# A decoder layer with routed experts: shared and expert tiles in another order, and the last sort spread differently

## What is computed

```python
probs = softmax(xf @ gate_w.T)
top_w, top_idx = top_k(probs, 4)
top_w = top_w / sum(top_w)
combine = zeros((T, 16)).at[rows, top_idx].set(top_w)
act = silu(einsum('td,ehd->teh', xf, w1)) * einsum('td,ehd->teh', xf, w3)
moe_out = einsum('ted,te->td', einsum('teh,edh->ted', act, w2), combine)
shared = silu(xf @ sw1.T) * (xf @ sw3.T) @ sw2.T
x = layernorm(x + moe_out + shared)
```

## Time and profile before

| | before |
|---|---|
| median of three runs | 969.44 us |
| lowest, highest | 969.18, 972.33 us |
| the profiled execution, device time | 975.99 us |
| its span in the trace | 973.7 us |
| mean granted clock of PE | 0.977 |
| busy: PE, PEld, DVE, ACT, POOL | 94%, 51%, 72%, 65%, 28% |

### The profile page before, as it was taken

The page is one execution under the profiler, slowest core; times in us unless marked ns, Lnnn a source line. Parts: engine busy times, 40 slices in busy tenths (PEclk is TensorE's granted clock), DMA queues, the critical chain, the costliest instruction groups (busy, mean ns, idle before and its releaser), DMA issues.

```text
span 973.7 us, 18713 instructions
## 1 busy us (share of the span) xinstructions
PE 914.7 (94%) x6751; PEld 497.8 (51%) x6751; DVE 703.9 (72%) x1121; ACT 635.3 (65%) x1354; POOL 273.9 (28%) x339
## 2 busy tenths in 40 slices
PE   8999999879999999999999999999989999799992
PEld 3455766434444444444444444444433577578771
DVE  2104889889999998898998989998897273211586
ACT  1323343238888888888888888877778755466662
POOL 1006675520000001020000110013444426655564
PEclk9999999869999999999999999999999999989997
DMA  9202956610444321010000000102335424445895
GB/s 328 66 0 82 119 146 133 121 66 3 128 137 132 100 65 26 8 29 24 24 13 24 25 12 24 31 13 89 96 111 170 130 67 122 136 125 160 267 298 172
DMA packets 69837, 93.05 MB, mean 96 GB/s; under 512 B 15254, under 2 KB 52632, under 8 KB 69686
## 3 DMA queue, kind: packets, MB, share of 16 engines
q1 hardware_dynamic: 62068, 70.06, 26.4%
q0 software_dynamic: 6928, 18.82, 5.3%
q10 hardware_dynamic: 752, 2.98, 1.7%
HBM read 50.34 MB, written 39.40 MB: 92 GB/s over the span
## 4 chain that ended last, share of the span: by engine, by line
PE 75%; DVE 11%; DMA 6%; issue 4%; ACT 3%; POOL 1%; SPq 0%; another core or an unknown queue 0%; POOLq 0%; ACTq 0%; DVEq 0%
PE psum L1338 20%; PE psum L1246 16%; PE psum L1324 9%; PE psum L1521 8%; DVE mpart L1675 7%; PE psum L1539 4%; DMA kparts_d<-region 3%; PE psum L1173 3%; PE psum L1140 3%; PE psum L1483 2%; ACT region L1088 2%; PE psum L1196 2%; PE psum L1298 2%; PE psum L1265 1%; PE psum L1360 1%
## 5 line engine op out<-in xcount | busy, mean ns | idle before, releaser
L1088 ACT ACTIVATE region<-psum 128x512 f32<-128x512 f32 (+1 forms) x832 | 448.3, 606 | 102.1 <-PE psum L1324 86.1
L1675 DVE TENSOR_REDUCE mpart<-psum 128x2 f32<-128x1024 f32 x384 | 462.0, 1222 | 37.5 <-PE psum L1246 31.6
L1338 PE MATMUL psum<-region 128*32 128x256 f32 (+1 forms) x3120 | 249.8, 392 | 2.3 <-ACT numT L987 0.6
L1246 PE MATMUL psum<-kstack,qstack 63*128 63x512 f32 (+1 forms) x1024 | 215.2, 448 | 13.4 <-DVE mpart L1675 11.8
L1246 PEld LDWEIGHTS psum<-kstack,qstack 63*128 63x128 f32 x1024 | 89.9, 188 | 184.7 <-issue 129.9
L1324 PE MATMUL psum<-qstack,kstack 64*128 64x512 f32 (+1 forms) x832 | 176.4, 410 | 1.6 <-ACT region L1088 1.0
L1324 PEld LDWEIGHTS psum<-qstack,kstack 64*128 64x128 f32 (+1 forms) x832 | 111.7, 183 | 18.0 <-ACT region L1088 11.3
L1338 PEld LDWEIGHTS psum<-region 128*32 128x32 f32 (+1 forms) x3120 | 62.1, 108 | 111.5 <-issue 80.8
L862 POOL TENSOR_TENSOR attnT<-num_c,den_c 128x512 f32<-128x512 f32 x7 | 9.1, 1303 | 331.6 <-DMA den_c<-den_d 331.6
L812 POOL DMA_INDIRECT given_d<-y_out,x_in x79 | 78.5, 993 | 65.2 <-ACT y_out L1068 47.4
L1521 PE MATMUL psum<-w_all,xT_in 128*128 x316 | 84.6, 391 | 6.4 <-issue 2.9
(11 more groups left out here) (266 smaller groups left out, 929.8 us busy)
## 6 DMA issues: line engine op xcount, KB each, us to landing
x_in<-sorted_d SPq DMA_DIRECT2D x79, 129.0 KB
sorted_d<-x_in SPq DMA_DIRECT2D x6, 1548.0 KB, 7.7
given<-given_d SPq DMA_DIRECT2D x16, 512.0 KB
qstack<-qparts_d SPq DMA_DIRECT2D x96, 64.0 KB, 2.3
qparts_d<-region SPq DMA_DIRECT2D x8, 512.0 KB, 2.8
kparts_d<-region SPq DMA_DIRECT2D x4, 800.5 KB, 14.1
kstack<-kparts_d SPq DMA_DIRECT2D x6, 400.2 KB, 10.3
kstack<-kparts_d ACTq DMA_DIRECT2D x6, 400.2 KB, 12.3
```

The lines of the kernel that those rows point to most:

```text
L1088: act.activation(prob[0:rows_of, s % 3, j, :], ring(n)[0:rows_of], ACT.Exp).then_inc(ring_read, 1)
L1246: mm = pe.matmul(bank(unit_bank(u) + side)[:, at * w:(at + 1) * w], qstack[rows_of, buffer(G), p, t * P:(t + 1) * P], kstack[rows_of, g * ...
L1338: mm = pe.matmul(bank(NUM_BANK)[VW * j:VW * (j + 1), q], vals[0:r, g, kt, j, :], prob[0:r, s % 3, j, q], start=(kt == 0 and half == 0), st ...
L1675: dve.tensor_reduce(mpart[:, G % 2, qt, :, p, n], both, X, ALU.max).then_inc(max_read, 1)
```

## The change

The list `WORK` gets another order. Before: six shared tiles, six expert tiles, eight pairs of a shared and an expert tile, then 42 expert tiles, and two late shared tiles among the last 25 items. After: three shared tiles, fourteen expert tiles, eleven shared tiles, and then the same 42 and the same rest. Item 28 is expert tile 14 in both, so that all items from 28 on are the same. In the first 28 items expert tile 0 moves from item 6 to item 3 and expert tile 13 from item 27 to item 16. The second edit puts the 16 scatters of the last stage into loops 14 to 29, one in each, in place of two in every three loops of 14 to 36.

```diff
-WORK = mixed("s" * 6 + "e" * 6 + "se" * 8 + "e" * 42 + "s" + "e" * 11 + "s" + "e" * 12, _shared, _expert)
+WORK = mixed("s" * 3 + "e" * 14 + "s" * 11 + "e" * 42 + "s" + "e" * 11 + "s" + "e" * 12, _shared, _expert)
...
-        SCATTER_AT = {14 + (3 * k) // 2: divmod(k, TPC) for k in range(TOPK * TPC)}
+        SCATTER_AT = {14 + k: divmod(k, TPC) for k in range(TOPK * TPC)}
```

## The result

| | before | after |
|---|---|---|
| median, us | 970.88 | 981.35 |
| runs, us | 969.18 to 974.96 | 979.45 to 985.11 |
| ratio to before, 95% interval | | 1.0093 [1.0065, 1.0120] |
| span of the profiled execution, us | 973.7 | 979.3 |

The forecast was 972.8 with a range of 964.0 to 977.5. The sign was right, the size wrong: the ratio is worth 9.0 us where 3.4 were forecast.

A forecast was written before the change was run, and what follows sets the result against it. PE, busy 94% of the span, was taken to bound the kernel. A 3.4 us stop at loop 0, with POOL's part set to nothing, gave 969.44 + 3.4 = 972.8 us; range 964.0 to 977.5.

The forecast's parts named there:

- The stop: At loop 0 PE waits for expert tile 0's load of `x_in`: 3.4 us, bounds 2.5 to 4.7.
- The sign named for it: In the profile after, the projection starts near 776.6 in place of 773.16; before 775 would prove the prediction wrong.
- The slots move with PE by the same 3.4 us.: Behind loop 0, the last chunk's norms, gate, ranks and slots hang on the projection and are 3.4 us late.
- no work is added: Front of the list: same tiles, scatters and reads of tile names and owners, so no work added or taken away.
- rival A: Behind loop 0's stop, PE's dense work runs at half clock, some 3.2 us more: 976.0 us; chance 0.20.
- Part 2, POOL: Last stage's scatters, one per loop: POOL is done sooner, but PE gains nothing; set to nothing in the sum.
- The time table: POOL's last sixteen scatters: done 33.5 us after the slots, at 837.5 on the old clock, 11.4 us sooner than before.
- rival B: Near loop 37, POOL's backlog makes PE wait 0.8 to 1.7 us for `x_in`: 974.5 us; chance 0.10.
- Rival C: PE's gaps of 830 to 860 and the fallen clock there, together 9.3 us, mostly go: 966 us, faster; chance 0.20.

The follow-up runs named there:

- four_shared_first: Changed kernel with four shared tiles in front instead of three, and ten behind the fourteen expert tiles; 973.70 us, 1.0009 of the kernel before.
- after_again: The changed kernel, unedited, run once more on the chip of the later runs; 981.88 us, 1.0093 of the kernel before.
- order_only: Changed kernel with the new tile order but the old spacing of the last chunk's scatters; 984.38 us, 1.0084 of the kernel before.
- fill_for_scatter: Changed kernel with a GpSimd fill in place of each of the sixteen last scatters, last chunk's rows left out; 0.9927 of the kernel before.
- marks_only: Changed kernel with the last chunk's eight marks but without its sixteen scatters, its rows left unsorted; 0.9956 of the kernel before.
- stop_alone: pairs_apart with three shared tiles in front instead of four and eleven behind instead of ten; 978.59 us, 1.0056 of the kernel before.
- pairs_apart_extra: pairs_apart with sixteen more scatters into scratch, one per loop in loops 50 to 65 between gives; 995.29 us, 1.0211 of the kernel before.
- pairs_apart: Changed kernel reordered to 4 shared, 7 expert, 10 shared, 49 expert tiles, two scatters per loop in loops 14 to 21; 971.67 us, 0.9976 of before.

## Why the prediction was wrong, step by step

- **The stop** (2.5 to 4.7 us, 3.4 taken). Right, and term by term: 1.2 us until the load is issued (1.3 forecast) and 2.16 from issue to PE's start (2.1). The twelve profiles with three shared tiles in front have 2.56 to 4.46, mean 3.4. Its cause, the load issued behind the attention stage's last scatter, is in the trace (SP's wait of 3.0 us), and with four shared tiles in front the stop is gone. The sign named for it held as well: the projection starts 773.76 - 766.31 = 7.45 us behind the entry, 776.7 on the clock of before, 776.6 forecast. What no sign looked for is growth behind it: from the projection's start to the last product it is 186.8 us against 182.3.
- **"The slots move with PE by the same 3.4 us."** This is the step that failed. They moved by 6.7 and, in the second profile, 4.6. The first missing term is the reads of owners, which I set to nothing with the words "no work is added": PE has to read before expert tile 0 and again before tile 4, and at items 3 and 7 these reads show as 1.04 + 0.83 us where they showed as 0.43 at item 6: 1.4 us. "No work is added" is true of the reads, but it says nothing of whether they stay covered. One loop later is enough to cover them better: in four_shared_first the read at item 4 shows as 0.42 us and the one at item 8 as nothing. The program fits that (the loop ahead of item 3's read is the only one of these without an `outer`, 0.60 us of PE's work), but no run tests it. The second missing term is the clock, which the sum had at nothing and only rival A counted.
- **Rival A, the clock.** True in after, 5.30 - 3.62 = 1.7 us, about half of the 3.2 I gave it, since half clock lasted some 3 us where I had supposed 6.8; not true in after_again, nor in order_only with a stop of 3.57 us. In the twelve profiles with the stop the granted clock of the first 41 us is below 1.00 in seven; in the eight without it, in none. So the fall goes with the stop but doesn't follow from its length: order_only had none behind 3.57, fill_for_scatter had one behind 2.68. Its length varies too: some 3 us in six of the seven, 7 in marks_only. By the rule of the Trainium skill ("TensorE: Matmul & The Clock Gate", HAM oscillation) that was cited under A, a gap of PE behind a DMA wait sends it back to half clock; the traces agree in seven of twelve. Sum of the front: 3.4 + 1.4 + 1.7 = 6.5 of after's 6.7; 2.9 + 1.4 = 4.3 of after_again's 4.6.
- **Part 2, POOL, "set to nothing".** For the spacing it is right, and a little cautious (0.9975). The time table was close: last scatter 31.8 us after the slots, 33.5 forecast. (Its subtraction from before is off by one: 849.91 - 837.5 is 12.4 us, not 11.4; nothing hangs on it.) No backlog reached PE: **rival B** didn't happen, PE has no idle time from 841 to 876. The stalls hold PE up while POOL goes on, which gives POOL time.
- **Rival C, the gaps go.** Wrong way round. The gaps stand where scatters and gives are dense, and shared tiles beside them don't help: 5.91 + 10.84 + 0.00 us idle in 110 us of after, 2.12 + 2.92 + 4.89 in before. Leaving the front out, after has 10.84 against 7.81, 3.0 more (after_again 9.39, 1.6 more; about 0.7 of after's is the tail of the idle time ahead of the slots, which before has in its front), and its clock in the stretch 41 to 75 is 0.90 in both, where before has 1.00 there and 0.90 in the next. So the same sixteen scatters cost somewhat more than before, and the gain that C hoped for didn't exist.
- **The remainder.** By the profiles after is 8.0 and after_again 957.89 - 764.61 - 186.2 = 7.1 us longer, of which 6.7 and 4.6 are in the front and 1.3 and 2.5 behind it. That closes with the 9.0 of the ratio to within a microsecond or two. The 7.8 us of stop_alone against the 4.7 of its profile doesn't close as well: either the front costs more in executions without a profile, or the intervals hide it. This is open.
- **The range** left out the sum of A and anything lost behind the front: forecast, clock and reads together would have given 976, and a stall or two more is outside 977.5. Carried to the median of the forecast, the measured ratio is 969.44 x 1.0093 = 978.5.

## What to carry to other kernels

A tile that is moved forward has to have its *first* load issued in time: compare the issue of that load with the new place before anything else, and put one or two independent tiles in front. Here four shared tiles instead of three were worth 8 us. Look also at every register read that the moved step makes on a bounding engine: here two of them showed with 1.4 us more in their new places. My reading is that a read shows when too little work is queued ahead of it; no run tests that.

Indirect DMAs of GpSimd have a price that no wait in the program shows: sixteen of them cost 13 us in after and 23 us in pairs_apart_extra, and fewer rows don't make one cheaper. Where no give is due they can be nearly free (0.5 us in 20 in pairs_apart), but they need not be (5.37 us in 15 in after). So it is worth trying to issue them while nothing else of that kind is due, and to measure it. With seven expert tiles and then ten shared ones, so that most scatters have no give beside them, the whole kernel ran at 0.9932 [0.9895, 0.9968] and 0.9976 [0.9960, 0.9992] of the kernel before, by one and by two scatters per loop. The old order with one scatter per loop reached 0.9975 [0.9954, 0.9996], so only the first of the two may be a gain by the order, and its interval overlaps the others'.

## What the runs showed of the hardware that I had not expected

- ACT stands still for 1 to 4 us, mostly ahead of `silu`, with its inputs complete, when GpSimd issues an indirect DMA each 1.3 us; PE and DVE then wait for it. The same occupancy of GpSimd with fills, and more traffic by plain DMAs (148 GB/s), do nothing of the kind. It isn't the destination, the row length or the number of rows. What holds ACT is open: the longest waits name only "remote" as releaser, a stall came beside gives alone as well (3.48 us at once), and scatters alone cost PE 0.5 us in 20 in one kernel and 5.37 in 15 in another.
- A stop of PE of 2.56 to 4.46 us is followed by half clock in seven of twelve profiles, for some 3 us in six and 7 in one, and by full clock in the other five.
- Reading four registers from SBUF takes PE's queue 0.76 to 1.43 us, median 1.12; how much shows depends on how full the queue ahead of it is, as far as items 3, 4, 6 and 7 tell (1.04, 0.42, 0.43 and 0.83 us).
